# GPS graph network on one core: edge chunks of 128 edges in place of 125

## The reference, cut to what matters

```python
dst = (3125 * uniform(50000) ** 2.0).astype(int32)         # then src, dst sorted by dst
# layer 0, six times
h = relu(x @ W1.T + b1) @ W2.T + b2
msg = segment_sum(h[src], dst, num_segments=3125)          # then a gated update of x
# layer 1, edge convolution
w = silu(edge_attr_8 @ fc_w0 / sqrt(8)) @ fc_w1 / 8        # wA, wB, wC, wD per edge
mid = products of w, h[src] and edge_attr_4
y = segment_sum(mid, dst, num_segments=3125)
```

## Time and profile before

| | |
|---|---|
| time, three runs | 4054.32, 4057.44, 4058.73 us; median 4057.44 us |
| span of the profiled execution | 4057.3 us, 61050 instructions |
| TensorE matmuls (PE) | 3711.8 us busy, 91% of the span |
| TensorE weight loads (PEld) | 3087.0 us, 76% |
| VectorE (DVE) | 2525.8 us, 62% |
| ScalarE (ACT) | 1533.3 us, 38% |
| GpSimd (POOL) | 758.0 us, 19% |
| TensorE clock granted, mean | 0.959 of full |

### The profile page before, as it was taken

One profiled execution on the slowest core, in us unless ns is written; L12 is line 12 of the kernel. 1 busy time (PEld: TensorE's weight loads), 2 busy tenths in 40 slices (PEclk: granted clock), 3 DMA queues, 4 the chain that ended last, 5 costly groups with the idle time before them and its releaser, 6 DMA issues. The chain is left out here.

```text
span 4057.3 us, 61050 instructions
## 1 busy us (share of the span) xinstructions
PE 3711.8 (91%) x18981; PEld 3087.0 (76%) x18981; DVE 2525.8 (62%) x5060; ACT 1533.3 (38%) x3578; POOL 758.0 (19%) x614
## 2 busy tenths in 40 slices
PE   5996879999999999999998799787999999779996
PEld 2554459989899899898997688655888888758884
DVE  7774755555555555555554555544777777577775
ACT  0363211121211211212112544334888886135553
POOL 0000000000000000000000200003888885012221
PEclk9997989999999999999999899898999999779998
DMA  1364112222222222222221211012333332411113
GB/s 41 64 102 87 48 50 78 87 67 85 76 79 86 74 80 87 67 85 76 79 85 40 66 30 31 13 41 61 93 93 93 94 93 68 177 44 35 38 35 116
DMA packets 297743, 288.61 MB, mean 71 GB/s; under 512 B 101485, under 2 KB 272847, under 8 KB 296806
## 3 DMA queue, kind: packets, MB, share of 16 engines
q1 hardware_dynamic: 233867, 208.29, 17.8%
q0 software_dynamic: 56576, 66.41, 6.4%
q10 hardware_dynamic: 7002, 10.15, 0.7%
HBM read 241.89 MB, written 42.47 MB: 70 GB/s over the span
## 5 line engine op out<-in xcount | busy, mean ns | idle before, releaser
L974 PE MATMUL bank<-a_wide,parts 125*128 125x448 f32 x4200 | 871.5, 367 | 0.1
L974 PEld LDWEIGHTS bank<-a_wide,parts 125*128 125x128 f32 x4200 | 785.7, 188 | 77.2 <-issue 10.1
L2205 POOL DMA_INDIRECT rows<-h_dram,src_t x400 | 493.5, 1234 | 124.1 <-DVE prod L2394 87.3
L2321 ACT ACTIVATE hot<-eq,ea 125x80 f32<-125x80 f32 x1600 | 413.2, 350 | 0.0
L949 POOL TENSOR_TENSOR nf_g<-nf,nf_g 128x896 fp32r<-128x896 f32 x42 | 94.5, 2249 | 1525.4 <-ACT nf_g L1112 1525.4
L1024 DVE CAST a_wide<-a_cols 125x2240 fp32r<-125x2240 bf16 x210 | 274.5, 1324 | 156.5 <-PE bank L974 141.0
L983 PE MATMUL bank<-nf_g,whh 128*128 128x448 f32 x1512 | 339.6, 369 | 0.0
L983 PE MATMUL bank<-msg,wc 128*128 128x448 f32 x1512 | 338.9, 368 | 0.0
L2247 PEld LDWEIGHTS bank<-prod,hot 125*80 125x80 f32 x2400 | 294.6, 150 | 54.1 <-issue 0.7
L2247 PE MATMUL bank<-prod,hot 125*80 125x128 f32 x2400 | 327.9, 273 | 0.0
L1117 ACT ACTIVATE msg<-bank 128x448 fp32r<-128x448 f32 x84 | 41.1, 542 | 702.6 <-PE bank L974 702.6
(11 more groups left out here) (431 smaller groups left out, 5894.4 us busy)
## 6 DMA issues: line engine op xcount, KB each, us to landing
a_cols<-a_dram SPq DMA_DIRECT2D x210, 546.9 KB
a_dram<-a_cols SPq DMA_DIRECT2D x15, 1250.0 KB, 10.9
w<-in_w SPq DMA_DIRECT2D x4, 2728.0 KB
deg_bc<-deg_dram SPq DMA_DIRECT2D x42, 224.0 KB, 6.1
gate_bc<-gate_dram SPq DMA_DIRECT2D x42, 224.0 KB, 3.2
rows<-h_dram,src_t POOLq DMA_INDIRECT x400, 4.2
w<-y_rows SPq DMA_DIRECT2D x12, 512.0 KB, 10.1
w<-in_w SPq DMA_DIRECT2D x5, 1024.0 KB
```

The source lines that it names most:

```text
L974: ins = nc.tensor.matmul(p_msg[f][:, 0:GW], parts[0:SPB, m, c * HB + k, f * 128:(f + 1) * 128], a_wide[u % 2][0:SPB, k, :], start=(c == 0 ...
L2205: nc.gpsimd.indirect_dma_start(out=rows[n % ITC][:, :], out_offset=None, in_=h_dram, in_offset=bass.IndirectOffsetOnAxis(ap=src_t[:, n:n + ...
L2321: ins = nc.scalar.activation(hot[:, q % 2, j, m, :], eq[:, q % 2, j, :], ACT.Copy, scale=ea4[:, q * UC + j, m:m + 1])
```

## The change

The constants go from `EC, NCH = 125, 400` to `128, 392`, so 98 units of 512 edges. 392 chunks of 128 hold 50176 edges; the last 176 are padding. A padded edge has source 0 and zero attributes. In `dst_t` its destination is 40000, past every tile and every window of 80 nodes, and in `dst_c`, from which the ranges of units and chunks are computed, it is the last real destination. Apart from the constants only the layout of the inputs is edited; every tile with `EC`, `NCH`, `NU` or `UE` in its shape changes with them.

```diff
-EC, NCH = 125, 400
+E, EC = 50000, 128
+NCH = 392
...
+    src_e, dst_e, dst_n = np.zeros(NCH * EC, np.int32), np.full(NCH * EC, int(NOWHERE) // KT, np.int32), np.full(NCH * EC, dst[-1], np.int32)
+    src_e[:E], dst_e[:E], dst_n[:E] = src, dst, dst
+    ea4, ea8 = np.zeros((NCH * EC, 4), np.float32), np.zeros((NCH * EC, 8), np.float32)
+    ea4[:E], ea8[:E] = i["edge_attr_4"], i["edge_attr_8"]
...
-        "src_t": c(src.reshape(NCH, EC).T),
-        "dst_t": c(dst.reshape(NCH, EC).T),
-        "dst_c": c(dst.reshape(NU, UE)),
+        "src_t": c(src_e.reshape(NCH, EC).T),
+        "dst_t": c(dst_e.reshape(NCH, EC).T),
+        "dst_c": c(dst_n.reshape(NU, UE)),
...
-        "ea4": c(np.asarray(i["edge_attr_4"]).reshape(NCH, EC, 4).transpose(1, 0, 2)),
-        "ea8": c(np.asarray(i["edge_attr_8"]).T),
+        "ea4": c(ea4.reshape(NCH, EC, 4).transpose(1, 0, 2)),
+        "ea8": c(ea8.T),
```

## The result

The changed kernel takes 4040.72 us (median of four runs, 4036.13 to 4044.58) against 4057.76 us before (four runs): ratio 0.9957, 95% interval 0.9943 to 0.9971. In a later comparison, on chip 1, it was 4038.85 us against 4058.23 us, ratio 0.9943 (0.993 to 0.9957). The forecast was 4036 us, with a range of 4028 to 4043 us. One more execution of the changed kernel on chip 3 took 4344.91 us at a granted clock of 0.823 and is left out of its median.

What follows compares the result with a forecast made beforehand. The prediction took TensorE to set the pace in the count matrix and the edge convolution. Its terms, -12.3 + 1.8 - 4.5 - 5.5 - 0.7 = -21.2 us from 4057.3 us, gave 4036 us, range 4028 to 4043 us.

Steps and rivals of the forecast that it cites:

- two units fewer: Edge convolution: 98 units in place of 100, at 6.16 us each, -12.3 us.
- each unit longer: Edge convolution: wider `hidden` and `weights` add 18 ns a unit (bounds 0 and 33), +1.8 us.
- gathers of 128 rows: Edge convolution, GpSimd: 1.0 us a gather against 1234 ns, gaining nothing since nobody waits for a gather.
- start of the edge convolution: `ea4` on 16 transfer engines in place of 5 ends VectorE's wait for loads earlier, -4.5 us (0 to -6.5).
- five turns fewer: Count matrix: 251 turns in place of 256, at 1.1 us each, -5.5 us (-3.5 to -6.0).
- setup: Setup: `hot_lo` covers fewer columns, -0.4 us, and the wait for `dst_c` shortens, -0.3 us; together -0.7 us.
- The slope from the last tiles, 1.19: Count matrix: upper bound on a turn's cost, (4.20 - 1.83) / 2 = 1.19 us; the lower was 0.70 us.
- GpSimd as the bound: Edge convolution, rival: GpSimd paces from 1.235 us a gather; at 1.33 us the kernel takes about 4073 us; chance 0.05.

Runs made afterwards that it cites:

- the clearing in halves: Changed kernel with `acc` cleared in two halves, by GpSimd and VectorE, in place of GpSimd alone: 4035.6 us; on chip 3, 4108.44 us.
- the run with the load in two: Kernel before, chunks of 125, with the load of `ea4` cut into 112 and 13 partitions: 4057.21 us, ratio 0.9996 (0.9987 to 1.0005).
- the run with 800 columns: Changed kernel with GpSimd clearing 800 columns of a spare tile ahead of each gather, on chip 3: 4177.28 us, ratio 1.0232 to before.

## Why the prediction was right, step by step

| step | forecast, us | measured in the traces, us |
|---|---|---|
| two units fewer | -12.3 | -12.3 (12.6 with 0.3 at the start) |
| each unit longer | +1.8 | +1.0 (6.160 against 6.150, 98 times) |
| gathers of 128 rows | 0 at 1.0 us each | 0 at 0.95 us |
| start of the edge convolution | -4.5 | -2.3 |
| five turns fewer | -5.5 | -5.65 |
| setup | -0.7 | -1.5 |
| sum | -21.2 | -20.8 |

The sum is right with one term off by half and two small ones that made up for most of it; that they did is luck. The steps that carry most of it, the units and the turns, came out by their own mechanism. The spans differ by 20.4 us. The medians differ by 17.0 us in the first comparison and 19.4 in the second; the phases between the count matrix and the edge convolution, which move by up to 7.3 us between executions, can cover what is between these and the sum.

*The start.* "What is late next is GpSimd's clearing of `acc`" was right, but I had it act through the one-hots, which wait for it by a semaphore, and put the loss at half a microsecond. It acts on VectorE's first copy after the loads, which has no such wait, so this copy, the weights of the first `hidden` and `hidden` itself all stay behind the clearing. The wait itself moved by 5.6 us in the first trace and by 4.5, the forecast, in the second; the copy ended at 11.25 us in both, so the 1.2 us between the two landings made no difference to what followed. The first products were forecast at 19.95 us after the clearing's start and came at 22.11; with the clearing in halves they came at 19.25. The reading that `ea4` and not `bout` is the late load was shown by the run with the load in two.

*A turn.* Tile 0 has 23 turns in place of 24 and ends 1.18 us sooner, tile 5 1.31, tile 17 1.17 (4.19 to 3.02). The mean over five is 1.13. The slope from the last tiles, 1.19, was the better of the two bounds. It is a mean and no constant: with chunks of 126, one turn fewer in all, the count matrix is 1.6 us shorter.

*Each unit.* 10 ns, inside 0 to 33. `hidden` grew by 5 ns and the eight loads by 3 ns each, 29 in all, and two thirds of it stay hidden.

*Setup.* `dst_cf` starts at 4.98 us and not at 6.17, after a wait of 3.25 us in place of 4.44. The load landed 1.2 us sooner, where I had bounded it at 0.8. Not all of that is due to 98 partitions in place of 100: with 400 chunks of 128, which keeps the 100, `dst_cf` starts at 5.43 us, and in the two runs that leave the setup of before as it was at 5.66 and 5.58.

*The rivals.* GpSimd as the bound did not come true; the run with 800 columns shows that it does bound at 1.91 us a chunk, and that it would from 1.54 stays argued. But the side on which the change makes the kernel slower did occur, on chip 3, by a mechanism that is none of the rivals: neither gather time nor loads, but signals of TensorE that come late. Its cause is open. Spacing the gathers in other ways, and a trace of the kernel before there, were not tried.

## What to carry to other kernels

A wait for several loads names the one issued last; which one is late is read from the DMA share in windows of a microsecond, and a partition count without a large divisor up to 16 is the first suspect (here 125, with a share of 0.33, against shares near 1 with 126 and 128). When a wait is shortened, look for what else runs in the stretch into which the work moves, here a GpSimd clearing beside a VectorE copy, not only for semaphores. A long instruction that ends with another engine's, at the same time in every trace, is the sign. And measure a change of 0.5% on more than one chip: this one was 0.4 and 0.6% faster in two comparisons and 0.7% slower on chip 3.

## What the runs showed of the hardware that was not expected

- A VectorE copy of f32 from SBUF to SBUF took 3.71 us in place of 0.37 while one GpSimd clearing ran, and 2.55, 2.00 and 1.69 where it began later. It ended each time 0.2 us after the clearing. With the clearing in pieces of 1.4 us two copies took 1.40 and 1.54. A VectorE clearing beside GpSimd's was not held (5.53 us beside 5.57).
- An indirect gather's time on GpSimd falls with the partition count: 1234 ns for 125 rows, 1105 for 126, 951 for 128. The software queue moved 56576 packets before, 30976 with 126 and 24192 after, for about the same data (66.41, 66.41 and 66.15 MB).
- On chip 3 TensorE's increments came in bursts in one phase, half of them over 1.1 us late, with a hole of 6.25 us at the place shown, and the changed kernel took 71 us more in that phase; the phases ahead of it and behind it took what they did elsewhere, within their spread. Elsewhere two traces of one kernel agree in that phase to 0.7 us.
